# Two graph layers on one core: the diagonal product of the graph numbers starts later, and the last pairs of rows run in another order

## The chip, the cores and the metric

The kernel runs on one core of a Trainium2 chip. The metric is the device time of one execution in microseconds (us), and of several executions the median. TensorE multiplies matrices (a matmul's weights are loaded beside the matmul before it), VectorE and ScalarE do elementwise work, GpSimd does small elementwise work here, and SyncE (SP) issues the DMAs. Each engine works through its own queue in order, and the engines wait for each other's semaphores.

## The reference

x is 2048 x 256, adj is a 2048 x 2048 matrix of zeros and ones. The first layer is graph attention with a gated second branch; the second is attention inside each of 32 graphs, whose bounds stand in ptr. Cut to what matters:

```
h   = relu(layernorm(x))
hs  = h @ W_sa;  s = hs @ a_left [:, None] + hs @ a_right [None, :]
e   = where(adj != 0, exp(-leaky_relu(s, 0.01)), 0)
x_a = e / (sum(e) + 1e-5) @ hs
x_b = adj @ (h @ W_gcnb) + b_gcnb
ga, gb = sigmoid([adj @ h, h] @ Wa.T + ba), sigmoid([adj @ h, h] @ Wb.T + bb)
x1  = x + sigmoid(ga * x_a + gb * x_b)

h1   = relu(layernorm(x1))
q, k, v = h1 @ Wq.T + bq, h1 @ Wk.T + bk, h1 @ Wv.T + bv
mask = graph_id[:, None] == graph_id[None, :]
sc   = (where(mask, q @ k.T / 16, 0) + 2 * adj) * where(mask, 1, -1e6)
out  = x1 + (softmax(sc) * mask) @ v
```

## The kernel before

The 2048 nodes are 16 tiles of 128, or 8 pairs of tiles. Every product of 32-bit numbers is made from 16-bit halves: a high half (made on ScalarE), a low half (the rest, made on VectorE or GpSimd), and three matmuls (high x high, high x low, low x high).

**Start.** `h` is made and turned, then multiplied with the weights (`times_weights`, `times_w_sa`), and `sums` adds up the second branch of the first block of 512 columns (`pair_sums` in the first tiles). Meanwhile VectorE makes `gid`, each node's graph number, and GpSimd's `gid_diag` is the product of the identity with it (L584, 2048 columns); TensorE's `spread_gid` (L1173) uses it much later, in sweep 0, and waits there for `norm_1_made` 3 and `graphs_made` 6. Around 32 us VectorE reduces the first layer's scores to a minimum (L1665), copies the s columns for a transpose (L1667, L1668), reduces the turned minimum (L1670), and makes the low half of `wsa` (L1672). TensorE turns the minimum (L1341), broadcasts it (L1344), turns the s columns (L1076), and goes on with `times_w_sa(0)` (L1053, `three_products`). Then `hd_low` (L1706) and `keep_b` (L1713 copies `tails`, L1714 makes `xb`) empty the banks of PSUM. `hd_low` of all pairs, `keep_b`, and L1761 have their places in VectorE's queue by hand.

**Sweeps 0 to 3.** In sweep k the engines build the attention weights of 512 rows pair by pair (`raw`, `high` on ScalarE, `mask`, `low` on VectorE) and TensorE's `attend` multiplies them with `hd`; `sums` of the next sweep lie between. At the head of sweep k + 1 the rows are finished: `denominators` (with `ga`, L1874), `keep_a`, `mix`, `tanh_mix`, `add_mix` (`add_only`, then `new_moments` for the layer norm), `inv_new_deviation` on GpSimd, `shifts`, and `normalize` on ScalarE with `h1_low` on GpSimd. DMA transposes on SP's queue (`turn_h1`) turn each pair's h1; each waits for `h1_low` of its pair.

**The last pairs.** After pair 5 of sweep 3 every engine follows a list written out by hand. It holds the last 4 tiles of `attend`, the finish of the last 4 tiles of rows (12 to 15), and the second layer's attention, pair by pair: `keys` and `values` (TensorE) wait for the transposes of the pair; `keys_high`, `keys_low`, `values_high`, `keep_values` (which makes `lift`) and `values_low` (GpSimd) keep them; `scores` multiplies; `maxima` (L1958, L1964) gives the row's shift; `exponents` and `turn_p`, `pT_high`, `pT_low` give the weights, `gather` (L1259) multiplies with the values, `outer_part` and `row_sums` (GpSimd) sum up the rest, and `results` (for the last pair `results_last`, L1987) write `o_sb`, which SP stores. These lists are what the change rewrites. A step waits for the numbers of its semaphores: `keys(p)` for the low half of the keys of pair p - 1, `values(p)` for `lift` of pair p - 1, `scores(p)` for the low half of its own pair and, below pair 3, for `keep_a` of row p, since it takes over that bank.

Of the kernel before, what the change touches and what calls it, by code (L numbers as in the profile page):

```python
# [10 lines left out]
ALU = mybir.AluOpType  # L11
# [19 lines left out]
def two_graph_layers(nc, x, adj, adj_t, W_sa, W_saT, a_col, W_gcnb, b_gcnb, gate_w, gate_b, ptr,  # L31
# [4 lines left out]
    NT = N // P  # L36
    KT = D // P
    CT = 4
# [14 lines left out]
    with ExitStack() as ctx:  # L53
# [3 lines left out]
        def sem(name):  # L57
            return ctx.enter_context(nc.semaphore(name))
# [211 lines left out]
        norm_1_summed = sem("norm_1_summed")  # L270
        norm_1_made = sem("norm_1_made")
        inv_1_made = sem("inv_1_made")
# [256 lines left out]
        def _(eng):  # L529
# [53 lines left out]
            eng.wait_ge(graphs_made, 5)  # L583
            eng.tensor_tensor(gid_diag, ident_b[:, :].rearrange("p (a n) -> p a n", a=1).broadcast_to([P, NT, P]),  # L584
# [3 lines left out]
            eng.tensor_tensor(ninv_1[:, :], nsq_1[:, :], half_neg[:, 0:4], ALU.pow).then_inc(inv_1_made, 1)  # L588
# [62 lines left out]
            eng.wait_ge(scale_1_made, SCALES)  # L651
            h1_low(4)
            outside(LAST)
            values_low(0)
            h1_low(5)
            values_low(1)
            inv_new_deviation(CT * LAST, CT * LAST + 2)
            outer_part(0)
            values_low(2)
            outer_part(1)  # L660
            outer_part(2)
            row_sums(0)
            inv_new_deviation(CT * LAST + 2, NT)
            h1_low(6)
            row_sums(1)
# [3 lines left out]
            outer_part(4)  # L669
            h1_low(7)  # L670
            row_sums(3)
            values_low(4)
            values_low(5)
            row_sums(4)
            outer_part(5)
            outer_part(6)
            row_sums(5)
            row_sums(6)
            outer_part(7)
            values_low(6)  # L680
            values_low(7)
            row_sums(NQ - 1)

        @block.scalar
        def _(eng):
# [265 lines left out]
            values_high(1)  # L951
            keep_a(LAST, 0, 2)
            tanh_mix(LAST, 0, 2)
            keys_high(1)
            exponents(0, 0)
            values_high(2)
            exponents(0, 1)
            keep_a(LAST, 2, CT)
            keys_high(2)
            normalize(6)  # L960
            pT_high(0)
            tanh_mix(LAST, 2, CT)
            values_high(3)
            exponents(1, 0)
            exponents(1, 1)
            keys_high(3)
            keys_high(4)
            pT_high(1)
            exponents(2, 0)
            normalize_tile(7, 0)  # L970
            exponents(2, 1)
            keys_high(5)
            pT_high(2)
            exponents(3, 0)
            normalize_tile(7, 1)
            values_high(4)
            exponents(3, 1)
            exponents(4, 0)
            exponents(4, 1)
            values_high(5)  # L980
            pT_high(3)
            pT_high(4)
            keys_high(6)
            exponents(5, 0)
            exponents(5, 1)
            keys_high(7)
            pT_high(5)
            exponents(6, 0)
            exponents(6, 1)
            values_high(6)  # L990
# [42 lines left out]
        def _(eng):  # L1033
# [142 lines left out]
            def norm_1():  # L1176
                eng.wait_ge(sq_1_made, 4)
                eng.matmul(L[:, 0, 0:4], ones[:, :], sq_1[:, :], start=True, stop=True).then_inc(norm_1_summed, 1)
# [211 lines left out]

            values(0, 0)
            values(0, 1)
            attend(LAST, NT - 4, (0, 1))
            attend(LAST, NT - 3, (0, 1))
            values(1, 0)
            values(1, 1)
            attend(LAST, NT - 2, (0, 1))
            attend(LAST, NT - 1, (0, 1))
            attend(LAST, NT - 4, (2, 3))
            values(2, 0)  # L1400
            values(2, 1)
            scores(0)
            keys(1)
            attend(LAST, NT - 3, (2, 3))
            attend(LAST, NT - 2, (2, 3))
            attend(LAST, NT - 1, (2, 3))
            keys(2)
            scores(1)
            values(3, 0)
            values(3, 1)  # L1410
            turn_p(0)
            scores(2)
            keys(3)
            values(4, 0)
            keys(4)
            gather(0)
            turn_p(1)
            values(4, 1)
            scores(3)
            keys(5)  # L1420
            turn_p(2)
            gather(1)
            scores(4)
            values(5, 0)
            values(5, 1)
            keys(6)
            gather(2)
            turn_p(3)
            turn_p(4)
            scores(5)  # L1430
            values(6, 0)
            values(6, 1)
            gather(3)
            keys(7)
            scores(6)
# [67 lines left out]
        def _(eng):  # L1503
# [278 lines left out]
            def norms_1():  # L1782

                eng.wait_ge(norm_1_summed, 1)
# [5 lines left out]
            def scales_1():  # L1790
                eng.wait_ge(inv_1_made, 1)
# [266 lines left out]
            keep_values(1)  # L2058
# [3 lines left out]
            keep_values(2)  # L2062
            maxima(0)
            add_mix(LAST, 0, 2)
            keys_low(1)
            denominators(LAST, 2, CT)
            shifts(NT - 4, NT - 2)
            mix(LAST, 2)
            mix(LAST, 3)
            keys_low(2)  # L2070
            maxima(1)
            keep_values(3)
            maxima(2)
            add_only(LAST, 2, CT)
            pT_low(0)
            new_moments(LAST, 2, CT)
            keys_low(3)
            shifts(NT - 2, NT)
            results(0)
            keys_low(4)  # L2080
            pT_low(1)
            maxima(3)
            keep_values(4)
            keys_low(5)
            maxima(4)
            results(1)
            pT_low(2)
            keep_values(5)
            results(2)
            pT_low(3)  # L2090
            pT_low(4)
            maxima(5)
            keys_low(6)
            results(3)
            keep_values(6)
            maxima(6)
            keys_low(7)
            pT_low(5)
            keep_values(7)
            maxima(7)  # L2100
            results(4)
            pT_low(6)
            results(5)
# [90 lines left out]
```

## Time and profile before

| | us |
|---|---|
| median of 3 executions | 231.44 (230.99 to 233.67) |
| profiled execution, its own time | 232.15 |
| profiled execution, span of the instructions | 230.2 |
| TensorE busy / VectorE / ScalarE / GpSimd | 217.0 / 190.2 / 161.5 / 68.3 |
| mean granted clock of TensorE | 0.992 of full speed |

The span runs from the first to the last instruction; the execution's own time is 1.95 us longer. Busy times are sums over the span and can overlap between the engines. An idle time in brackets behind a row is that of the engine just before it, with the instruction that released it.

### The profile page before, as it was taken

To read this page: it belongs to the slowest core of one execution; us is meant where nothing else is said; L and a number is where in the kernel's file an instruction comes from. 1 tells how busy PE (TensorE), PEld (TensorE's weight loads), DVE (VectorE), ACT (ScalarE), POOL (GpSimd) and SP (SyncE) were. 2 spreads that over 40 slices of the span, in tenths; PEclk is the share of its full clock that TensorE was granted. 3 is DMA by queue.
4 is the path that set the end of the run, shared out by engine and by line. 5 is a ranking of instruction groups with operands and counts; after the bars stand their busy time and mean duration, and the time that the engine had idled before them with its cause. 6 is when DMAs were issued, how large, how long until landed. Compare 5 with 4: busy or idle time off the path is not lost.

```text
span 230.2 us, 5297 instructions
## 1 busy us (share of the span) xinstructions
PE 217.0 (94%) x1974; PEld 187.9 (82%) x1976; DVE 190.2 (83%) x481; ACT 161.5 (70%) x310; POOL 68.3 (30%) x114
## 2 busy tenths in 40 slices
PE   7999989999999999999999999999999989899980
PEld 7878878888888888888888888888788769788850
DVE  2889898989996975699999499987599949899891
ACT  3779735799967434975782795669999845999660
POOL 4643860000026000001800001732124472267470
PEclk9999999999999999999999999999999999999996
DMA  6999499006989300824410000001203131012733
GB/s 194 353 373 382 127 358 362 7 0 211 291 272 391 118 3 0 299 93 157 129 56 3 1 1 3 1 3 39 52 3 68 26 63 30 4 24 42 191 109 99
DMA packets 28796, 28.43 MB, mean 124 GB/s; under 512 B 10593, under 2 KB 20577, under 8 KB 28769
## 3 DMA queue, kind: packets, MB, share of 16 engines
q1 hardware_dynamic: 28080, 27.81, 37.2%
q8 instruction: 16, 0.26, 0.5%
q10 hardware_dynamic: 688, 0.27, 0.5%
q14 instruction: 12, 0.09, 0.1%
HBM read 23.88 MB, written 2.10 MB: 113 GB/s over the span
## 4 chain that ended last, share of the span: by engine, by line
PE 62%; DVE 20%; issue 6%; ACT 5%; DMA 3%; POOL 1%; SPq 1%; DVEq 0%; ACTq 0%; POOLq 0%
PE bank_b L1105 21%; PE bank_a L1053 9%; PE bank_a L1129 9%; PE bank_a L1131 9%; PE bank_a L1133 9%; DVE e_lo L1728 2%; DVE adjt L1919 2%; DVE e_slot L1722 2%; DMA adjt<-in_x 2%; ACT adjt L844 2%; PE bank_l L1045 1%; DVE st6b L1897 1%; DMA adjt<-adjt 1%; DVE x_all L1889 1%; DVE adjt L1999 1%
## 5 line engine op out<-in xcount | busy, mean ns | idle before, releaser
L1131 PE MATMUL bank_a<-hd,e_hi 128*128 128x257 f16 x256 | 70.2, 274 | 0.0
L1129 PE MATMUL bank_a<-hd,e_hi 128*128 128x257 f16 x256 | 69.6, 272 | 0.1
L1133 PE MATMUL bank_a<-hd,e_lo 128*128 128x257 f16 x256 | 69.5, 271 | 0.0
L1105 PE MATMUL bank_b<-hb,adjt 128*128 128x259 f16 (+1 forms) x512 | 66.5, 273 | 0.5 <-DVE hb L1539 0.3
L1105 PEld LDWEIGHTS bank_b<-hb,adjt 128*128 128x128 bf16 x512 | 49.3, 97 | 7.9 <-DVE xb L1714 0.5
L735 ACT ACTIVATE e_hi<-e_slot 128x1024 f16<-128x1024 f32 x32 | 33.6, 1050 | 26.6 <-PE bank_a L1133 15.4
L1722 DVE SCALAR_TENSOR_TENSOR e_slot<-e_slot,adjt 128x1024 f32<-128x1024 f32 x32 | 39.0, 1218 | 8.6 <-ACT e_slot L728 8.6
L1728 DVE SCALAR_TENSOR_TENSOR e_lo<-e_slot,e_hi 128x1024 f16<-128x1024 f32 x32 | 39.0, 1218 | 4.9 <-ACT e_hi L735 4.9
L728 ACT ACTIVATE e_slot<-s_row,nbias 128x512 f32<-128x512 f32 x64 | 42.3, 709 | 0.2
L593 POOL TENSOR_TENSOR rs_all<-veb,half_neg 128x2 f32<-128x2 f32 x8 | 7.4, 930 | 72.8 <-DVE veb L1902 72.8
L1129 PEld LDWEIGHTS bank_a<-hd,e_hi 128*128 128x128 f16 x256 | 24.7, 96 | 4.1 <-issue 0.3
L1133 PEld LDWEIGHTS bank_a<-hd,e_lo 128*128 128x128 f16 x256 | 25.2, 98 | 3.3
L1131 PEld LDWEIGHTS bank_a<-hd,e_hi 128*128 128x128 f16 x256 | 24.6, 96 | 3.7
L844 ACT ACTIVATE adjt<-x_all,nb_all,rs_all 128x256 f32<-128x256 f32 (+1 forms) x32 | 16.6, 591 | 0.4 <-DVE nb_all L1912 0.4
L616 POOL TENSOR_TENSOR adjt<-adjt 128x512 f16<-128x512 f32 x8 | 9.3, 1164 | 20.7 <-ACT adjt L844 20.7
L1053 PE MATMUL bank_b<-w_v,adjt 128*128 128x257 f16 x96 | 12.1, 273 | 1.5 <-DVE lift L1933 1.5
L817 ACT ACTIVATE xa<-bank_a,ga 128x256 f32<-128x256 f32 x16 | 6.4, 475 | 9.6 <-DVE ga L1874 9.6
L1053 PE MATMUL bank_l<-adjt,w_qk 128*128 128x256 f16 x96 | 11.8, 273 | 0.2 <-DMA adjt<-adjt 0.2
L588 POOL TENSOR_TENSOR ninv<-nsq,half_neg 128x4 f32<-128x4 f32 x1 | 1.9, 1930 | 33.6 <-DVE nsq L1788 33.6
L1053 PE MATMUL bank_a<-wb,x_all 128*128 128x262 f16 x96 | 11.8, 274 | 0.0
L1053 PE MATMUL bank_a<-wsa,x_all 128*128 128x256 f16 x96 | 11.6, 272 | 0.0
L1053 PEld LDWEIGHTS bank_b<-w_v,adjt 128*128 128x128 f16 x96 | 9.1, 97 | 3.0 <-issue 1.7
(232 smaller groups left out, 363.4 us busy)
## 6 DMA issues: line engine op xcount, KB each, us to landing
adjt<-in_adj_t SPq DMA_DIRECT2D x16, 1024.0 KB, 9.0
x_all<-in_x SPq DMA_DIRECT2D x4, 512.0 KB, 5.4
out<-adjt SPq DMA_DIRECT2D x16, 128.0 KB, 1.8
adjt<-in_x SPq DMA_DIRECT2D x3, 512.0 KB, 7.3
diag<-in_adj SPq DMA_DIRECT2D x16, 64.0 KB, 3.8
adjt<-in_x SPq DMA_DIRECT2D x2, 256.0 KB, 3.7
e_slot<-in_L_gnn_W_gcnb ACTq DMA_DIRECT2D x1, 256.0 KB, 3.9
e_slot<-in_W_saT SPq DMA_DIRECT2D x1, 256.0 KB, 4.1
```

Of the source, the lines that this page charges most:

```text
L593: eng.tensor_tensor(rs_all[:, first:last], veb[:, r0:r1], half_neg[:, 0:r1 - r0], ALU.pow) \
L616: eng.tensor_tensor(h1n16[:, p % ROWS, :, 1, :], h1[:, p % 2, :, :], h1n16[:, p % ROWS, :, 0, :], ALU.subtract).then_inc(h1_lo_made, 1)
L728: ins = eng.activation(slot_words(g)[:, n * CW:(n + 1) * CW], s_row[:, k * CW:(k + 1) * CW], ACT.Exp, scale=SLOPE - 1.0, bias=nbias[:, j:j ...
L735: eng.activation(high_words(g), slot_words(g), ACT.Copy, scale=E_SCALE).then_inc(hi_ready, 1)
L844: eng.activation(into, x1_all[:, i * D:(i + 1) * D], ACT.Relu, scale=rs_all[:, i:i + 1], bias=nb_all[:, i:i + 1]).then_inc(h1_ready, 1)
L1053: mm = eng.matmul(bank, left(kk, a), right(kk, b), start=(kk == 0 and a + b == 0), stop=(kk == KT - 1 and a == 1))
L1105: eng.matmul(B[:, r % 2, 0:cols], adjt_block(k, j, r), hb16[:, j, part, 0:cols], start=(j == 0 and part == 0), stop=(j == NT - 1 and part ...
L1129: eng.matmul(A[:, r, 0:D + 1], high, hd16[:, j, 0, 0:D + 1], start=(j == 0), stop=False, skip_group_check=True)
L1131: eng.matmul(A[:, r, 0:D + 1], high, hd16[:, j, 1, 0:D + 1], start=False, stop=False, skip_group_check=True)
L1133: mm = eng.matmul(A[:, r, 0:D + 1], low, hd16[:, j, 0, 0:D + 1], start=False, stop=(j == NT - 1), skip_group_check=True)
L1722: eng.scalar_tensor_tensor(out=slot_words(g), in0=slot_words(g), scalar=1.0, in1=adjt_words(k, 2 * q, 0, PW), op0=ALU.min, op1=ALU.mult) \
L1728: eng.scalar_tensor_tensor(out=low_words(g), in0=slot_words(g), scalar=E_SCALE, in1=high_words(g), op0=ALU.mult, op1=ALU.subtract) \
```

## The change

GpSimd waits for `norm_made` 6, which VectorE signals with L1697, before it makes `gid_diag`. Two semaphores are merged into others that count the same instructions. The order of the last pairs is another one on TensorE, ScalarE, VectorE and GpSimd; `normalize`, `keep_a` and `add_mix` are split into their parts at some places, and the steps stay the same. SP's queue is unchanged.

```
@@ gpsimd @@
             eng.wait_ge(graphs_made, 5)
+            eng.wait_ge(norm_made, 6)
             eng.tensor_tensor(gid_diag, ident_b..., gid..., ALU.mult).then_inc(graphs_made, 1)
             eng.wait_ge(norm_1_made, 3)
-            eng.tensor_tensor(ninv_1[:, :], nsq_1[:, :], half_neg[:, 0:4], ALU.pow).then_inc(inv_1_made, 1)
+            eng.tensor_tensor(ninv_1[:, :], nsq_1[:, :], half_neg[:, 0:4], ALU.pow).then_inc(inv_made, 1)
@@ norm_1 (tensor), norms_1 and scales_1 (vector) @@
-  ... .then_inc(norm_1_summed, 1)          -  eng.wait_ge(norm_1_summed, 1)     -  eng.wait_ge(inv_1_made, 1)
+  ... .then_inc(norm_summed, 1)            +  eng.wait_ge(norm_summed, 5)       +  eng.wait_ge(inv_made, 5)
```

The four lists before stand in the listing above; after the change they read, in order:

```
GpSimd:  outside(LAST) h1_low(4) inv_new_deviation(12, 14) outer_part(0) h1_low(5) values_low(0)
         outer_part(1) row_sums(0) row_sums(1) values_low(1) inv_new_deviation(14, 16) h1_low(6)
         outer_part(2) values_low(2) h1_low(7) row_sums(2) outer_part(3) values_low(3) values_low(4)
         values_low(5) outer_part(4) outer_part(5) row_sums(3) row_sums(4) outer_part(6) row_sums(5)
         values_low(6) outer_part(7) values_low(7) row_sums(6) row_sums(7)
ScalarE: keep_a(LAST, 0, 1) keep_a(LAST, 1, 2) tanh_mix(LAST, 0, 2) keys_high(1) keep_a(LAST, 2, 3)
         keep_a(LAST, 3, 4) keys_high(2) normalize_tile(6, 0) exponents(0, 0) exponents(0, 1)
         tanh_mix(LAST, 2, 4) keys_high(3) values_high(1) pT_high(0) exponents(1, 0) exponents(1, 1)
         keys_high(4) values_high(2) pT_high(1) normalize_tile(6, 1) normalize_tile(7, 0)
         exponents(2, 0) exponents(2, 1) normalize_tile(7, 1) keys_high(5) pT_high(2) values_high(3)
         exponents(3, 0) exponents(3, 1) keys_high(6) values_high(4) values_high(5) exponents(4, 0)
         pT_high(3) keys_high(7) exponents(4, 1) exponents(5, 0) pT_high(4) exponents(5, 1)
         pT_high(5) values_high(6) exponents(6, 0) exponents(6, 1) values_high(7) pT_high(6)
         (then as before)
TensorE: attend(tiles 12 to 15, rows 0, 1) values(0) attend(tiles 12 to 15, rows 2, 3) keys(1) keys(2)
         scores(0) values(1) keys(3) turn_p(0) scores(1) values(2) keys(4) gather(0) values(3, 0)
         turn_p(1) scores(2) values(3, 1) keys(5) scores(3) values(4) gather(1) turn_p(2) scores(4)
         keys(6) values(5, 0) turn_p(3) values(5, 1) gather(2) keys(7) scores(5) values(6) turn_p(4)
         scores(6) gather(3) turn_p(5) values(7) (then as before: scores(7) gather(4) turn_p(6) ...)
VectorE: denominators(LAST, 0, 2) mix(0) mix(1) denominators(LAST, 2, 4) add_only(LAST, 0, 2)
         new_moments(LAST, 0, 2) keys_low(1) shifts(12, 14) mix(2) maxima(0) mix(3) keep_values(1)
         keys_low(2) maxima(1) add_only(LAST, 2, 4) pT_low(0) keep_values(2) keys_low(3)
         new_moments(LAST, 2, 4) keys_low(4) shifts(14, 16) keep_values(3) maxima(2) results(0)
         pT_low(1) maxima(3) keep_values(4) results(1) pT_low(2) keys_low(5) maxima(4) keys_low(6)
         keep_values(5) results(2) pT_low(3) maxima(5) keys_low(7) keep_values(6) pT_low(4) maxima(6)
         results(3) pT_low(5) keep_values(7) maxima(7) (then as before: results(4) pT_low(6) ...)
```

## Rows read from the trace of the kernel before

Each row of a timeline has its start, its duration, the engine, the line, the operation, what it writes and reads, and how many instructions.

**Rows 1.** The page: busy time and share of the span of each engine.

```profile
PE 217.0 (94%) x1974; PEld 187.9 (82%) x1976; DVE 190.2 (83%) x481; ACT 161.5 (70%) x310; POOL 68.3 (30%) x114
```

**Rows 2.** TensorE's waits from 44 us on, longest first.

```profile
PE bank_b L1053 <- DVE lift L1933: 1.5, 1, 1.5
```

**Rows 3.** Timelines of GpSimd and VectorE, the product and its neighbours.

```profile
30.56 3.61 POOL L584 TENSOR_TENSOR z_same<-ident_b,gid 128x2048 bf16<-128x2048 bf16 x1 [2.07 <-DVE onehot L1556]
67.75 1.93 POOL L588 TENSOR_TENSOR ninv<-nsq,half_neg 128x4 f32<-128x4 f32 x1 [33.58 <-DVE nsq L1788]
...
31.91 2.29 DVE L1667 COPY s_cols<-hc 128x16 f32<-128x16 f32 x1
34.12 0.18 DVE L1668 COPY s_cols<-hc 128x32 f32<-128x32 f32 x1
34.22 0.27 DVE L1670 TENSOR_REDUCE rm<-bank_l 1x1 f32<-1x128 f32 x1
34.42 0.73 DVE L1672 SCALAR_TENSOR_TENSOR wsa<-e_slot,w_mul,wsa 128x512 f16<-128x512 f32 x1
```

**Rows 4.** Timeline of TensorE from 32 to 36 us.

```profile
32.56 0.27 PE L1341 MATMUL bank_l<-ident,rm 128*1 128x128 f32 x1
...
34.54 0.38 PE L1344 MATMUL bank_l<-rm,ones 1*128 1x1 f32 x2 [0.82 <-DVE rm L1670]
...
35.20 2.79 PE L1053 MATMUL bank_a<-wsa,x_all 128*128 128x256 f16 x24
```

**Rows 5.** Timeline of VectorE from 37 to 42 us.

```profile
37.59 0.15 DVE L1697 TENSOR_TENSOR norm<-norm_sq,norm_inv 128x1 f32<-128x1 f32 x1
...
39.20 0.23 DVE L1713 COPY tails<-bank_b 128x71 f32<-128x71 f32 x1 [0.39 <-PE bank_b L1115]
...
41.05 0.22 DVE L1761 TENSOR_TENSOR hd<-dp_s,hd 128x16 f16<-128x16 f32 x1
```

**Rows 6.** Timelines of GpSimd and VectorE around 213 us.

```profile
212.05 2.28 POOL L621 TENSOR_TENSOR adjt<-adjt 128x512 f16<-128x512 f32 x2
...
212.98 0.74 DVE L1969 SCALAR_TENSOR_TENSOR adjt<-bank_a,adjt 128x256 f16<-128x256 f32 x2
```

**Rows 7.** Timeline of TensorE in the last pairs.

```profile
180.90 0.83 PE L1053 MATMUL bank_b<-w_v,adjt 128*128 128x257 f16 x6
...
198.81 0.84 PE L1217 MATMUL bank_a<-adjt 128*128 128x128 f16 x12 [1.12 <-DVE adjt L1919]
199.49 1.47 PE L1053 MATMUL bank_l<-adjt,w_qk 128*128 128x256 f16 x12
200.80 0.83 PE L1053 MATMUL bank_b<-w_v,adjt 128*128 128x257 f16 x6
201.46 1.47 PE L1053 MATMUL bank_l<-adjt,w_qk 128*128 128x256 f16 x12
...
203.43 0.38 PE L1226 MATMUL bank_a<-ident,adjt 128*128 128x128 f32 x2
203.65 0.72 PE L1053 MATMUL bank_b<-w_v,adjt 128*128 128x257 f16 x5
```

**Rows 8.** Timelines of GpSimd and VectorE: ga beside GpSimd's work and without it.

```profile
195.07 1.16 POOL L621 TENSOR_TENSOR adjt<-adjt 128x512 f16<-128x512 f32 x1
...
160.93 0.22 DVE L1874 SCALAR_TENSOR_TENSOR ga<-rden,norm,gates 128x4 f32<-128x4 f32 x1
...
195.27 0.97 DVE L1874 SCALAR_TENSOR_TENSOR ga<-rden,norm,gates 128x2 f32<-128x2 f32 x1
```

**Rows 9.** The chain that ended last, at the last pair's transposes.

```profile
210.16 1.12 POOL adjt L616
...
212.53 2.81 DMA adjt<-adjt
```

**Rows 10.** Timelines of TensorE and VectorE: the last scores and the last result.

```profile
219.19 0.51 PE L1217 MATMUL bank_a<-adjt 128*128 128x128 f16 x6
...
225.05 0.47 DVE L1987 SCALAR_TENSOR_TENSOR adjt<-bank_a,rz,x_all 128x256 f32<-128x256 f32 x1
```

More of the change, by code:

```diff
@@ L668, in _ @@
             values_low(3)
[L669 to L671 removed]
             values_low(4)
             values_low(5)
+            outer_part(4)
+            outer_part(5)
+            row_sums(3)
             row_sums(4)
[L675 removed]
             outer_part(6)
             row_sums(5)
+            values_low(6)
+            outer_part(7)
+            values_low(7)
             row_sums(6)
[L679 to L682, printed above, removed]
+            row_sums(7)
         @block.scalar
@@ L1177, in norm_1 @@
                 eng.wait_ge(sq_1_made, 4)
-                eng.matmul(L[:, 0, 0:4], ones[:, :], sq_1[:, :], start=True, stop=True).then_inc(norm_1_summed, 1)
+                eng.matmul(L[:, 0, 0:4], ones[:, :], sq_1[:, :], start=True, stop=True).then_inc(norm_summed, 1)
             def keys(p):
@@ L1388, in _ @@
                         attend(k, 1)
+            attend(LAST, NT - 4, (0, 1))
+            attend(LAST, NT - 3, (0, 1))
+            attend(LAST, NT - 2, (0, 1))
+            attend(LAST, NT - 1, (0, 1))
             values(0, 0)
             values(0, 1)
[L1393 to L1398, printed above, removed]
             attend(LAST, NT - 4, (2, 3))
[L1400 to L1403, printed above, removed]
             attend(LAST, NT - 3, (2, 3))
@@ L1406, in _ @@
             attend(LAST, NT - 1, (2, 3))
+            keys(1)
             keys(2)
-            scores(1)
[L1409 to L1414, printed above, removed]
+            scores(0)
+            values(1, 0)
+            values(1, 1)
+            keys(3)
+            turn_p(0)
+            scores(1)
+            values(2, 0)
+            values(2, 1)
             keys(4)
             gather(0)
+            values(3, 0)
             turn_p(1)
+            scores(2)
+            values(3, 1)
+            keys(5)
+            scores(3)
+            values(4, 0)
             values(4, 1)
-            scores(3)
-            keys(5)
+            gather(1)
             turn_p(2)
-            gather(1)
             scores(4)
+            keys(6)
             values(5, 0)
+            turn_p(3)
             values(5, 1)
-            keys(6)
             gather(2)
-            turn_p(3)
-            turn_p(4)
+            keys(7)
             scores(5)
@@ L1432, in _ @@
             values(6, 1)
+            turn_p(4)
+            scores(6)
             gather(3)
-            keys(7)
-            scores(6)
             turn_p(5)
@@ L2061, in _ @@
             mix(LAST, 1)
-            keep_values(2)
-            maxima(0)
-            add_mix(LAST, 0, 2)
+            denominators(LAST, 2, CT)
+            add_only(LAST, 0, 2)
+            new_moments(LAST, 0, 2)
             keys_low(1)
-            denominators(LAST, 2, CT)
             shifts(NT - 4, NT - 2)
             mix(LAST, 2)
+            maxima(0)
             mix(LAST, 3)
+            keep_values(1)
             keys_low(2)
             maxima(1)
+            add_only(LAST, 2, CT)
+            pT_low(0)
+            keep_values(2)
+            keys_low(3)
+            new_moments(LAST, 2, CT)
+            keys_low(4)
+            shifts(NT - 2, NT)
             keep_values(3)
             maxima(2)
[L2074 to L2078, printed above, removed]
             results(0)
-            keys_low(4)
             pT_low(1)
```

75 lines of the change are left out of this document (38 added, 37 removed).

## The prediction

> **What bounds the kernel now.** I first read the busy shares on the page, to see that TensorE works 94% of the span [rows 1]. So only idle time on TensorE, the start and the end can be saved. Next come TensorE's waits from 44 us on, to see how few they are: the largest are 1.5 us, for `lift` of VectorE, and 1.1 us, for the low half of the keys [rows 2, 7]. Both lie in the last pairs. The third view is the timeline of GpSimd and VectorE around 30 us. The diagonal product runs 3.61 us from 30.56, and a copy of 16 columns that starts at 31.91 takes 2.29 us and ends at 34.20, just when the product ends [rows 3]. TensorE's timeline shows who pays: the broadcast of the minimum starts at 34.54 after 0.82 us idle, released by the reduction that stands behind the copy [rows 4]. From 44 us to about 180 us TensorE has no wait that the view lists, so what it wins at 34 us should reach the end.
>
> **Part 1, the product held back.** `gid_diag` now waits for `norm_made` 6, which L1697 signals. The copy then costs what its neighbour of 32 columns does, 0.18 us [rows 3]. The reduction L1670 is limited instead by TensorE's transpose L1341, 32.56 + 0.27 = 32.83 [rows 3, 4]. Reduction (0.27) and wsa's low half (0.73) then end at about 33.85, where they ended at 35.15 before. TensorE reaches the broadcast at 34.54 - 0.82 = 33.72, when its minimum is ready (33.1), and `times_w_sa(0)` (35.20 before, behind 0.66 us of broadcast and transpose) comes at 34.38, later than 33.85 [rows 4]. The whole 0.82 us goes, and nothing takes its place: gain 0.82 us.
>
> Where does the product land? L1697 stood at 37.59 [rows 5]. VectorE's chain in front of it gains the 0.82 us of TensorE's transpose of the s columns and somewhat more, so I put it at 36.3 and the product at 36.4 to 40.0. Bounds: free if nothing on VectorE wants the port then; at worst the product's own 3.61 us, less the time nothing waits. What stands there on VectorE is `hd_low` and `keep_b`, which read PSUM and one SBUF tensor. Steps of that form are not slowed: two `pT_low` take 0.74 us inside 2.28 us of GpSimd work [rows 6]. The next step with two SBUF tensors is L1761, at 41.05 - 0.82 = 40.23, 0.2 us after the product [rows 5]. I take zero. Behind the new wait GpSimd has nothing until `ninv_1` at 67.75, after 33.58 us of idleness, and TensorE's `spread_gid`, which uses the product, also waits for `norm_1_made` 3, the very thing that released `ninv_1` [rows 3]. SP's queue is not touched. The merged semaphores (`norm_summed` 5, `inv_made` 5) count the same instructions: zero.
>
> One step under the product has no twin in the trace: the copy of `tails` from PSUM (L1713, 39.20) [rows 5]. If it took the port, it would wait from 38.38 to 40.04, and TensorE's later wait for `xb` with it: 1.66 us. I take zero, for the other PSUM readers of rows 6. The Trainium skill ("VectorE: DVE Perf Modes", Mode 2×_2P) says that a copy with a PSUM source can't use both ports, since PSUM has one VectorE read port; by that rule this risk is nil; no row here shows it for a copy.
>
> **Part 2, the last pairs.** The set of steps is the same on every engine (`add_mix`, `normalize`, `keep_a` are only split), so TensorE's work between its first changed step at 180.90 and `scores(7)` at 219.19 is fixed. From start to start [rows 7]: scores 0.68, keys 1.31, half of values 0.66 (0.11 a matmul of 257 columns), gather 203.43 - 201.46 - 1.31 = 0.66, turn 0.22. There are 48 matmuls of `attend` (5.3), 16 halves of values (10.6), 7 keys (9.2), 7 scores (4.7), 6 turns (1.3), 4 gathers (2.6): 33.7 us. 38.29 us pass, so TensorE stands idle 4.55 us there. That is the ceiling of part 2.
>
> What makes the idleness? GpSimd's long steps read SBUF, and VectorE's steps with two SBUF tensors stand still beside them: `ga` took 0.22 us alone and 0.97 us when it met `values_low` [rows 8]. That `ga` holds up `keep_a`, `mix` and the keys of pair 2, for which `scores(2)` waited 1.12 us [rows 7]. The 1.5 us wait is that of `values(1)`, which stands so early that `keep_values(0)` isn't done [rows 2].
>
> For the rest I laid the four queues side by side: each step starts when its engine is free and its semaphores are there 0.04 us after the signal, durations as in the timelines of this profile, and a step with two SBUF tensors on VectorE and a reader on GpSimd exclude each other. Laid out so, the old order ends at 225.99, where the trace has its last result at 225.05 + 0.47 = 225.52 [rows 10], and `scores(7)` at 219.66, where it was 219.19. Without the exclusion it would end at 222.9, 2.6 us too early: the port is a real part of the loss.
>
> The new order gives TensorE: `attend` of rows 0, 1 to 183.56 (the low half that its third step needs is there at 181.8, the step comes at 182.2), `values(0)` to 184.89, rows 2, 3 to 187.55, keys 1 and 2 to 190.17, `scores(0)`, `values(1)`, keys 3, then 0.23 us of waiting for pair 0's exponents. VectorE has `ga` at 186.2 and 188.2 with GpSimd idle from 185.7 to 190.6; its steps are no longer blocked until 195.4, and then by 0.1 us. `lift` of pair 0 comes at 185.9, `values(1)` only at 190.84. TensorE reaches keys 6 at 204.96. Their transposes depend on `h1_low(6)`, at 200.39 in the new order. A pair of transposes lands 4.05 us after `h1_low` ends (210.16 + 1.12, then 212.53 + 2.81 = 215.34) [rows 9]: at 205.63, a wait of 0.68 us. Keys 7 wait 0.13 us in the same way. All in all 1.04 us idle, `scores(7)` at 180.90 + 33.74 + 1.04 = 215.68. That is 3.51 us earlier. From there to the last result it was 6.33 us [rows 10]; laid out it is 6.39, since GpSimd's order of the last sums differs. Gain 3.45 us.
>
> Bounds of part 2: all idleness gone, 4.5 us; or the 4.05 us of a transpose grow, each of them one for one (at 4.9 instead of 4.05 the end is 0.85 later).
>
> By the Trainium skill ("SBUF — State Buffer", Who interferes with whom) a `tensor_scalar` from SBUF to SBUF can hold both ports too. In the new order this meets the small step `veb` of tiles 14, 15 at 199.05, beside `values_low(1)`: 0.25 us later there, 0.06 us at the end, so the gain would be 4.21 instead of 4.27. No row here shows it for a `tensor_scalar`; for the copy of rows 3 the trace agrees.
>
> **The sum.** 0.82 + 3.45 = 4.27 us. The profiled execution took 232.15 us (span 230.2), so 227.9; it was 0.71 us above the median, 231.44, so for the median 227.2.
>
> **Rivals.**
> - All waits go. The layout made the old order 0.47 us too long, so it may overstate the new one too. With no idleness at all: 0.82 + 4.49 = 5.31, 226.1. Against it: the transposes' latency is a measured floor.
> - Held back in vain. The copy's 2.29 us ends with the product, which speaks for the port; if it stood still for another reason, 0.82 stays: 228.0. If the `tails` copy takes the port at the new place: 227.2 + 1.66 = 228.9.
> - The new order makes waits of its own. ScalarE has two runs without a break (197.4 to 201.3 and 201.9 to 206.6), and each wait of one pair holds the next pair's behind it. If this gives back 2 of the 3.45 us: 229.2.
> - Slower. One mechanism: the layer norm of tiles 13 to 15 now stands on ScalarE behind the exponents and the turn of pair 1, and `new_moments` of tiles 14, 15 on VectorE behind the turn of pair 0. Is that chain late, `h1_low(6)` and (7) are late, the transposes land late, and keys 6 and 7 stop TensorE one for one. Against it: the layout has them late by only 0.68 and 0.13 us. It decides from 4.3 us of further lateness on; at 5.3 us the time is 232.5.
>
> **How the numbers follow.** A difference under 2% (4.6 us) is about what a measurement of this kernel can't tell from none; 226.8 is the bound. Chances: forecast 227.2 (226.4 to 228.2) 0.56; all waits go 0.12; in vain or the copy blocked 0.13; new waits 0.15; slower 0.04. The range 226.0 to 229.8 leaves out the slow case and the edges of the two neighbours. Faster by over 2%: the 0.12 and nearly half of the forecast's own range, 0.35. Slower by over 2% (236.1) needs 9 us of stalls: 0.02. The rest, 0.63.
>
> **What the changed profile would show.** Right: the copy L1667 near 0.2 us; no idle time before the broadcast L1344; the product at about 36.4, 3.6 us long, `tails` copies beside it at 0.23 us; both `ga` of the last pairs at 0.2 us; about 1 us of TensorE waits from 180 us to `scores(7)`, most before keys 6 and 7 and released by DMA; `scores(7)` 4.3 us earlier. Wrong: a long L1713 or L1706 under the product, a wait of TensorE for `xb` above 0.2 us; waits for ScalarE's exponents or keys' high halves; `h1_low(6)` more than 1 us behind the end of pair 1's exponents; or a lower granted clock after a stall.

## The result and the profile after

The changed kernel takes 228.28 us (median of 4 runs, 227.96 to 228.85), the kernel before 231.57 us (median of 4 runs beside it). The ratio is 0.985, interval 0.980 to 0.989: 3.3 us faster, inside the range, 1.1 us more than the 227.2 us forecast. The profiled execution took 228.31 us, span 226.5.

The page of the changed kernel, busy time by engine. TensorE's work is the same (216.7 us against 217.0), VectorE's is 4.3 us less [rows 1]. It has as many instructions as before (481), so its steps only stand still less.

```profile
PE 216.7 (96%) x1974; PEld 189.0 (83%) x1976; DVE 185.9 (82%) x481; ACT 161.4 (71%) x310; POOL 68.5 (30%) x114
```

VectorE and GpSimd of the changed kernel around the place the product left, and around its new one (timelines; the code stands two lines further down than before for VectorE and TensorE, so L1667 is now L1669):

```profile
32.15 0.16 DVE L1669 COPY s_cols<-hc 128x16 f32<-128x16 f32 x1
32.23 0.18 DVE L1670 COPY s_cols<-hc 128x32 f32<-128x32 f32 x1
33.11 0.28 DVE L1672 TENSOR_REDUCE rm<-bank_l 1x1 f32<-1x128 f32 x1 [0.70 <-PE bank_l L1343]
33.32 0.73 DVE L1674 SCALAR_TENSOR_TENSOR wsa<-e_slot,w_mul,wsa 128x512 f16<-128x512 f32 x1
...
38.35 0.23 DVE L1715 COPY tails<-bank_b 128x71 f32<-128x71 f32 x1 [0.63 <-PE bank_b L1117]
...
40.20 0.29 DVE L1763 TENSOR_TENSOR hd<-dp_s,hd 128x16 f16<-128x16 f32 x1
```
```profile
36.79 3.61 POOL L583 TENSOR_TENSOR z_same<-ident_b,gid 128x2048 bf16<-128x2048 bf16 x1 [8.05 <-DVE norm L1699]
```

The copy fell from 2.29 to 0.16 us [rows 3], and the reduction behind it is ended by TensorE's transpose, as forecast. The product stands at 36.79 to 40.40. Both things that lie under it are to be read here: the copy of `tails`, which reads PSUM, takes 0.23 us as before [rows 5], and the step with two SBUF tensors that just touches its end takes 0.29 instead of 0.22 us.

TensorE of the changed kernel at the same place (timeline). No idle time stands before the broadcast, and `times_w_sa` comes 0.83 us earlier [rows 4], though the transpose in front (32.80) was 0.24 us later than in the run of before:

```profile
32.80 0.27 PE L1343 MATMUL bank_l<-ident,rm 128*1 128x128 f32 x1
...
33.89 0.38 PE L1346 MATMUL bank_l<-rm,ones 1*128 1x1 f32 x2
...
34.37 2.78 PE L1055 MATMUL bank_a<-wsa,x_all 128*128 128x256 f16 x24
```

TensorE's waits from 44 us on (in total, how many, the longest), and its timeline in the last pairs:

```profile
PE bank_l L1055 <- DMA adjt<-adjt: 2.1, 2, 1.4
PE bank_a L1228 <- ACT adjt L867: 0.5, 1, 0.5
PE bank_l L1237 <- ACT adjt L867: 0.3, 1, 0.3
PE bank_b L1246 <- DVE adjt L1978: 0.2, 1, 0.2
```
```profile
193.27 0.44 PE L1228 MATMUL bank_a<-ident,adjt 128*128 128x128 f32 x2 [0.49 <-ACT adjt L867]
...
205.46 0.72 PE L1055 MATMUL bank_l<-adjt,w_qk 128*128 128x256 f16 x5 [0.72 <-DMA adjt<-adjt]
...
210.56 1.48 PE L1055 MATMUL bank_l<-adjt,w_qk 128*128 128x256 f16 x12 [1.41 <-DMA adjt<-adjt]
...
216.97 0.83 PE L1219 MATMUL bank_a<-adjt 128*128 128x128 f16 x12
```

The waits for `lift` and for the low half of the keys [rows 2, 7] are gone. Three are left before `scores(7)` (216.97): `turn_p(0)` for the exponents, keys 6 and keys 7 for their transposes. The chain that ended last shows keys 7's (start, duration):

```profile
203.67 1.17 POOL adjt L615
204.85 1.19 SPq L510
206.09 4.42 DMA adjt<-adjt
210.56 1.48 PE bank_l L1055 x12
```

Before, the first and the last of these took 1.12 and 2.81 us [rows 9], and the link on SP 1.19 us as now. It is the DMA that is 1.61 us longer.

The last result (VectorE's timeline) comes at 222.93 + 0.48 = 223.41, where it was 225.52 [rows 10]: 2.11 us earlier. The span is 3.7 us shorter. The difference lies behind the last result, in SP's stores; two timelines, before and after:

```profile
214.14 12.69 SPq L464 DMA_DIRECT2D out<-adjt  x16
```
```profile
207.40 16.47 SPq L462 DMA_DIRECT2D out<-adjt  x16
```

Before, the last issue ends at 226.83, 1.31 us behind the last result; after, at 223.87, 0.46 us behind. From the last result to the end of the span it is 4.68 us before and 3.09 after. This isn't the change's doing: three of the experiments below keep the old order of the last pairs and have 3.1 us there (the first: span 228.7, last result 225.65). The profiled execution of before was 1.6 us longer behind its last result than theirs; why isn't shown.

### The profile page after: what moved, and what is told of

It is laid out like the page before. It is cut to its first block, busy times and chain, and to the rows that moved or that the text cites. A ratio compares the mean times of both kernels' runs of the same rounds, so it can differ in the third digit from the quotient of the medians.

```text
span 226.5 us, 5300 instructions
## 1 busy us (share of the span) xinstructions
PE 216.7 (96%) x1974; PEld 189.0 (83%) x1976; DVE 185.9 (82%) x481; ACT 161.4 (71%) x310; POOL 68.5 (30%) x114
## 4 chain that ended last, share of the span: by engine, by line
PE 82%; DVE 7%; issue 3%; POOL 2%; ACT 2%; DMA 2%; SPq 1%; DVEq 0%; POOLq 0%; ACTq 0%
PE bank_b L1107 25%; PE bank_a L1131 12%; PE bank_a L1133 12%; PE bank_a L1135 12%; PE bank_a L1055 9%; PE bank_a L1281 2%; DMA adjt<-adjt 2%; PE bank_l L1055 2%; PE bank_b L1055 2%; PE bank_l L1047 1%; DVE adjt L2001 1%; PE bank_a L1219 1%; PE bank_b L1149 1%; DVE adjt L1960 1%; DVE adjt L1933 1%
## 5 line engine op out<-in xcount | busy, mean ns | idle before, releaser
L1055 PEld LDWEIGHTS bank_l<-adjt,w_qk 128*128 128x128 f16 x96 | 9.2, 97 | 3.7 <-DMA adjt<-adjt 2.6
L1055 PEld LDWEIGHTS bank_a<-wb,x_all 128*128 128x128 f16 x96 | 9.2, 98 | 1.5 <-DVE norm_sq L1651 0.2
```

What stands on the lines that cost most here:

```text
L1055: mm = eng.matmul(bank, left(kk, a), right(kk, b), start=(kk == 0 and a + b == 0), stop=(kk == KT - 1 and a == 1))
```

## The experiments

Each time is the median, beside runs of the kernel before in the same job (231.22 us for the first four, 231.11 for the next four, 231.32 for the last three); ratios are to those, with the 95% interval in brackets. Each trace is of one execution, so a time in it can differ from the median.

**1 and 2. The two parts alone.** Part 1 alone is one line in the kernel before; part 2 alone is the changed kernel without it.

```diff
+            eng.wait_ge(norm_made, 6)
             eng.tensor_tensor(gid_diag, ident_b[:, :].rearrange("p (a n) -> p a n", a=1).broadcast_to([P, NT, P]),
```

> The kernel before with the held-back product alone. Theory of the port: the copy of 16 columns falls from 2.29 us to under 0.2, the idle 0.82 us in front of the broadcast is gone, and TensorE's first step of the last pairs comes 0.8 to 0.9 us earlier (180.90 before): time 0.8 us lower, 0.3%. The rest of the saving belongs to the new order. Rival, that the head start is given back later: the same head start at 44 us, but the last result not earlier than 225.3 us. Rival, that the product does harm at its new place: a tails copy or an xb step over 1 us long.

> The changed kernel without the wait that holds the product back. If the parts add up: about 2.5 us faster than before (3.3 less 0.8), the copy long again (about 2.3 us), 0.8 us idle before the broadcast, and in the last pairs the same waits as in the changed kernel (0.5, 0.7 and 1.4 us). Rival, that the parts need each other: no faster than 1.5 us.

Measured: part 1 alone 230.12 us, ratio 0.995 (0.992 to 0.999), so 1.1 us faster. Part 2 alone 228.50 us, 0.989 (0.985 to 0.993), 2.7 us faster. Both together were 3.3 us faster, less than the sum, 3.8; each interval is wider than that difference, so it isn't shown that the parts fail to add up. The traces say where something may go. Part 1 alone, VectorE's copy and TensorE's keys 7:

```profile
32.27 0.16 DVE L1668 COPY s_cols<-hc 128x16 f32<-128x16 f32 x1
```
```profile
215.50 1.49 PE L1054 MATMUL bank_l<-adjt,w_qk 128*128 128x256 f16 x12 [1.05 <-DMA adjt<-adjt]
```

Part 2 alone, the same two:

```profile
32.17 2.30 DVE L1668 COPY s_cols<-hc 128x16 f32<-128x16 f32 x1
```
```profile
210.50 1.49 PE L1054 MATMUL bank_l<-adjt,w_qk 128*128 128x256 f16 x12 [0.36 <-DMA adjt<-adjt]
```

The copy is short with the hold and long without it, in any order of the pairs. But keys 7 start at 210.50 without the hold and at 210.56 with it: in the changed kernel the wait there is 1.05 us longer. Part 2 alone, the chain at the last transpose:

```profile
205.96 1.19 SPq L510
207.20 3.25 DMA adjt<-adjt
```

With the hold this transpose is issued at 206.09, 1.11 us earlier, so GpSimd and SP had kept the head start. The transfer lost it: 4.42 us against 3.25. Experiments 6 and 7 show why. In part 1 alone the profiled execution gives the whole head start back at keys 7: its last result is at 225.65, against 225.52 before, which is the sign named for the first rival. The median is 1.1 us lower all the same, as the theory had it, so on where the head start of part 1 alone ends up trace and median disagree.

**3. The stores held back.** In the changed kernel SP issues the first stores at 207.40, before keys 7's transposes land. If the stores hold those up, then it helps to wait.

```diff
+            eng.wait_ge(h1_turned[1], turned(NQ - 1))
```

(on SP, between the last transposes and the first store)

> The changed kernel, and SP's queue waits for the last pair's transposes before the first store of a result. In the changed kernel the second transpose of the last pair landed 4.42 us after its issue, where 2.4 to 3.4 us was seen before, and the first stores were issued 1.3 us behind it. Theory of the collision: the stores' packets hold it up; now it lands within 2.9 us, keys(7) waits 0 to 0.2 us instead of 1.41, scores(7) comes 1.2 to 1.4 us earlier, and the time is 1.0 to 1.4 us below the changed kernel's. Rival, the DMA queue is slow by itself there (a fetch of instructions, or two transposes behind one another): still 3.5 us or more to landing, and the time unchanged. Rival, the stores come too late: transposes on time, but the span's end 1 us or more further behind the last result.

Measured: 227.92 us, ratio 0.985 (0.981 to 0.988), as the changed kernel. The stores' row on SP and TensorE's keys 7:

```profile
210.35 13.34 SPq L462 DMA_DIRECT2D out<-adjt  x16
```
```profile
210.38 1.48 PE L1056 MATMUL bank_l<-adjt,w_qk 128*128 128x256 f16 x12 [1.21 <-DMA adjt<-adjt]
```

No store is under way any more and the second transpose still lands 4.1 us after its issue. That the stores delay it is refuted.

**4. The copy as a reduction.** In the kernel before, the two copies are written as sums over an axis of one element; the product stays where it was.

```diff
-            eng.tensor_copy(s_cols[:, 0, 0:NT], hc[:, :, 2]).then_inc(s_parts_made, 1)
-            eng.tensor_copy(s_cols[:, 2:4, 0:NT], across(hc[:, :, 2], [P, 2, NT])).then_inc(s_parts_made, 1)
+            eng.tensor_reduce(s_cols[:, 0, 0:NT], hc[:, :, 2:3], AX, ALU.add).then_inc(s_parts_made, 1)
+            for n in (2, 3):
+                ins = eng.tensor_reduce(s_cols[:, n, 0:NT], hc[:, :, 2:3], AX, ALU.add)
+            ins.then_inc(s_parts_made, 1)
```

> The kernel before with the product where it was, and the two copies of the s columns made by additions over an axis of one element, which read one tensor and give the same numbers (three instructions instead of two). Theory of the port: a reduction needs no second port; each takes under 0.25 us beside the product, the 0.82 us wait before the broadcast is gone, time 0.7 to 0.8 us lower than before, just as in the run with the product held back. Rival, any read of SBUF on VectorE is held up by the product, or the columns' stride is what is slow: the first reduction takes over 1 us, and the time doesn't change.

Measured: 230.51 us, 0.998 (0.994 to 1.001). GpSimd's product and VectorE beside it:

```profile
31.20 3.61 POOL L584 TENSOR_TENSOR z_same<-ident_b,gid 128x2048 bf16<-128x2048 bf16 x1 [2.09 <-DVE onehot L1556]
```
```profile
32.53 0.17 DVE L1667 TENSOR_REDUCE s_cols<-hc 128x16 f32<-128x16 f32 x1
32.62 0.26 DVE L1669 TENSOR_REDUCE s_cols<-hc 128x16 f32<-128x16 f32 x2
...
33.71 1.65 DVE L1674 SCALAR_TENSOR_TENSOR wsa<-e_slot,w_mul,wsa 128x512 f16<-128x512 f32 x1
```

The same 16 columns move in 0.17 us in the middle of the product: it is the kind of instruction that stood still, not the data or the place. But the next step, with two SBUF tensors, now meets the product and takes 1.65 instead of 0.73 us; it ends at 35.36, and TensorE waits 0.50 us for it. Of the 0.82 us saved, the trace gives 0.50 back, so on TensorE a cheaper copy alone wins about 0.3 us: the product has to go from there. The median is 0.7 us lower, as the theory forecast, but the interval reaches no change at all and doesn't tell 0.3 from 0.8. The Trainium skill ("SBUF — State Buffer", Who interferes with whom) says just this of the two: a reduction can't enter a mode with two ports and never contends, a step with two inputs in SBUF contends with GpSimd's reads. The trace agrees with both, 0.17 and 1.65 us.

**5. One swap on GpSimd.** In the kernel before, `values_low(2)` goes behind `outer_part(1)`, so that no long GpSimd step meets the second `ga`.

```diff
             outer_part(0)
-            values_low(2)
             outer_part(1)
+            values_low(2)
```

> The kernel before with one step moved on GpSimd: values_low(2) behind outer_part(1), so that it no longer runs beside the second ga of the last pairs. Theory of the port: that ga takes 0.22 us instead of 0.97, keep_a, the keys' halves of pair 2 and scores(2) come 0.7 us earlier, so TensorE's 1.12 us wait there falls to about 0.4; the other waits stay, and the last result is up to 0.7 us earlier if the last transposes don't take it back. Rival, ga is long for another reason (two tiny operands on partitions that ScalarE reads): it stays near 0.9 us and so does the 1.12 us wait.

Measured: 230.77 us, 1.000 (0.996 to 1.004). VectorE's two `ga` and TensorE's `scores(2)`:

```profile
188.78 0.74 DVE L1874 SCALAR_TENSOR_TENSOR ga<-rden,norm,gates 128x2 f32<-128x2 f32 x1
195.42 0.22 DVE L1874 SCALAR_TENSOR_TENSOR ga<-rden,norm,gates 128x2 f32<-128x2 f32 x1
```
```profile
198.21 0.84 PE L1217 MATMUL bank_a<-adjt 128*128 128x128 f16 x12 [0.38 <-DVE adjt L1919]
```

The second `ga` fell from 0.97 to 0.22 us and `scores(2)`'s wait from 1.12 to 0.38 us [rows 7, 8], so the cause of that wait is shown. In the profiled execution the last result comes 0.94 us earlier (224.58). But that execution (229.46 us) is the fastest of the twelve; the median is 0.3 us below the kernel before, and the ratio shows no gain. So what the wait's end is worth at the end of the kernel stays open.

**6 and 7. The instructions' fetch.** What is beside keys 7's transposes? In the views of the DMA queues there is one packet of instructions (queue 8) every 11 to 18 us from 180 us on. They are TensorE's: the waits put on its queue below move them against the work. The changed kernel from 207.6 to 208.2 us:

```profile
DMA packets 347, 0.10 MB, mean 163 GB/s; under 512 B 346, under 2 KB 346, under 8 KB 346
...
q1 hardware_dynamic: 346, 0.08, 67.6%
q8 instruction: 1, 0.02, 14.2%
```

Of 347 packets all but one are the transposes' small ones, and the one takes 14.2% of 16 x 0.6 us, 1.4 us of a DMA engine's time. To move it against the work I put waits that are always satisfied at TensorE's start: 24 in one kernel, 66 in the other.

```diff
+            for _ in range(24):
+                eng.wait_ge(consts_made, 1)
```

> The changed kernel with 24 waits more at TensorE's start, on a semaphore that is already there. They compute nothing; they move the places at which TensorE's instructions are fetched by 24 instructions, so each fetch comes about 1.3 us earlier. In the changed kernel one fetch (one packet on one DMA engine, near 208.2 us) falls together with the last pair's second transpose (its packets at 207.3 to 208.1), which then trickles on until 210.5. Theory of the fetch: here the packet comes near 206.9 us, still within the transposes, and the landing stays late (3.5 us or more after its issue) and the time within 0.5 us of the changed kernel. Rival, the transposes are slow there by themselves: the landing stays late in this and in the run with 66 waits.

> The same with 66 waits: the fetch comes about 3.6 us earlier, near 204.6 us, in the gap between the transposes of pairs 6 and 7. Theory of the fetch: the last transpose lands 2.4 to 2.9 us after its issue, keys(7) waits under 0.2 us instead of 1.41, and the time is 1.0 to 1.4 us below the changed kernel's. Rival, slow by themselves: landing 3.5 us or more, time unchanged. Rival, the fetch only moves onto pair 6's transposes: keys(6) waits over 1.5 us instead of 0.72, and the time doesn't change.

Measured: with 24 waits 228.9 us, 0.990 (0.987 to 0.993); with 66 waits 233.56 us, 1.009 (1.006 to 1.0125). So the second is 5.3 us slower than the changed kernel, where its expectation said 1.0 to 1.4 us faster. The waits weren't free. The broadcast before `times_w_sa` (33.89 in the changed kernel) stands at 34.53 and at 36.94, that is 0.64 and 3.05 us later (in the profiles with the hold and without these waits it stands anywhere from 33.60 to 34.11), so the packet (at 207.8 both times, where 206.9 and 204.6 were expected) is 0.8 and 3.2 us earlier against the work, not in the time of the trace. With 66 it hits another pair: keys 6's transposes land late and keys 7's in time. The chain of the kernel with 66 waits, and its DMA issues from 210 to 212 us, the last transpose among them (2.5 us to landing):

```profile
204.26 1.19 SPq L510
205.88 4.05 DMA adjt<-adjt
209.97 2.09 PE bank_l L1055 x12
```
```profile
adjt<-adjt SPq DMA_TRANSPOSE x1, 2.5
```

So the late landing went with the packet from one pair to the other: of the expectation for 66 waits, keys 7's part came true, and so did the last rival (keys 6 wait 2.19 us). Over the profiles of before, of the changed kernel and of experiments 1 to 7 (packet's start in windows of 0.2 us; issue of the transposes from SP's rows or in windows of 0.3 us; both in us), for the transposes of pairs 6 and 7:

| kernel | packet | late transposes: issue, landing after | the others of these pairs |
|---|---|---|---|
| before | 212.0 | 211.3: 3.4; 212.5: 2.8 | 2.4 to 2.5 |
| part 1 alone | 211.2 | 210.6: 3.5 | 2.4 to 2.5 |
| changed | 208.0 | 206.1: 4.4 | 2.4 to 2.6 |
| part 2 alone | 207.8 | 205.7: 4.0; 207.2: 3.3 | 2.4 to 2.5 |
| stores held back | 207.8 | 206.3: 4.1 | 2.4 |
| 24 waits | 207.8 | 206.7: 3.9 | 2.4 to 2.5 |
| 66 waits | 207.8 | 205.9: 4.0 | 2.4 to 2.5 |
| reduction | 210.0 | none under way | 2.4 to 2.5 |
| GpSimd swap | 209.4 | none under way | 2.4 to 2.5 |

In the two kernels where the packet falls between the pairs no transpose is late. The earlier pairs show the same. In the changed kernel the second transpose of pair 5 (issued at 194.94) meets the packet before; nothing waits for it yet, and keys 5 start at 199.73 without a wait. The row of its issue and the row of the packet (window 196.6 to 196.8 us):

```profile
adjt<-adjt SPq DMA_TRANSPOSE x1, 4.2
```
```profile
q8 instruction: 1, 0.02, 27.4%
```

The traces of all thirteen profiles hold 208 transposes. 30 of them landed 2.8 to 4.4 us after their issue, and with each of these a packet of queue 8 was under way between issue and landing. The other 178 took 2.4 to 2.6 us; only two of them meet such a packet, one in its own last 0.07 us, and for the other the packet is over (208.8) before SP is done issuing it (209.2). With the 66 waits that moved packet and lateness together, this shows the packet as the cause. It also shows what the landing follows. 26 of the 30 were issued before the packet began, from 0.6 to 2.4 us before, and all of these landed 2.0 to 3.1 us after the packet's start. So an earlier issue gains little there: without the hold the last transpose had 0.7 us from issue to packet, with it 2.0, and it landed at 210.5 in both. Why the landing takes 2.0 us or more from the packet's start isn't explained; the packet's own time is 0.9 to 1.4 us. The Trainium skill ("Runtime: NRT & Kernel Launch", Instruction fetch mechanics) says that each engine's sequencer fetches its instructions by DMA in blocks of 16 KiB, 256 instructions, and calls the cost mostly hidden; the row's 0.02 MB fits the block, the table doesn't fit "hidden": none of TensorE's listed waits is for instructions, but a transfer that it waits for is late.

The 66 waits cost more than their 3.05 us. TensorE stood still for 2.35 us before 209.97, and 0.7 us later its granted clock fell (windows of 1 us; behind the stretch PE, PEld, DVE, ACT and POOL busy, then the granted clock):

```profile
209.00:210.00 1.00, 0.03 (x1) 0.03 (x2) 0.95 (x6) 0.19 (x3) 0.97 (x1) 1.00 0.65 131
210.00:211.00 1.00, 1.00 (x8) 0.82 (x9) 0.00 (x0) 0.00 (x0) 0.00 (x0) 0.84 0.49 100
211.00:212.00 1.00, 1.00 (x6) 0.72 (x5) 0.00 (x0) 0.00 (x0) 0.00 (x0) 0.50 0.49 145
...
213.00:214.00 1.00, 1.00 (x6) 0.82 (x5) 0.85 (x2) 0.46 (x1) 0.46 (x1) 0.50 0.43 143
214.00:215.00 1.00, 1.00 (x10) 0.89 (x9) 0.30 (x1) 0.00 (x0) 0.69 (x1) 0.95 0.00 0
```

From about 210.7 to 214.1 it is 0.5, the 1.2 GHz level. Keys there take 2.09 instead of 1.48 us, half of values 1.50 instead of 0.83, the turn 0.63 instead of 0.38, the next half 1.08 instead of 0.83: 1.8 us together. With 3.05 at the start, 2.35 - 0.88 at keys 6 and -1.57 at keys 7 this makes 4.7 us; the last result is 4.6 us later (227.98).

**8 to 11. A third order with slack before the transposes.** If the transposes' landing is what is left, TensorE should have other work while it waits. The steps of the last pairs in a third order, the hold kept (TensorE's list, cut to the parts that matter; the other three lists are rearranged to suit):

```diff
+            turn_p(2)
             values(4, 0)
             values(4, 1)
             gather(1)
-            turn_p(2)
             scores(4)
-            keys(6)
             values(5, 0)
-            turn_p(3)
             values(5, 1)
+            keys(6)
+            turn_p(3)
             gather(2)
-            keys(7)
             scores(5)
             values(6, 0)
             values(6, 1)
             turn_p(4)
+            keys(7)
             scores(6)
```

> The changed kernel with the four lists of the last pairs in a third order, the same steps: laid out as in the prediction, but with the transposes taken once at 4.05 us and once at 5.2 us, and an order looked for that ends early with either. The normalized tiles of pairs 6 and 7 and their low halves stand further in front, keys(6) and keys(7) further behind. If late transposes are what the changed kernel still pays (0.72 + 1.41 us), TensorE waits under 0.5 us in all between 180 us and scores(7), the last result comes 1.3 to 2 us earlier than the changed kernel's 223.4, and the time is 1.2 to 2 us lower, about 226.5. Rival, the layout is wrong in what it doesn't know (ScalarE without a gap): new waits for exponents or halves of over 1 us, and no gain.

Measured: 226.17 us (225.78 to 226.32), 0.977 (0.973 to 0.982). That is the best of all kernels here. The list has no wait of TensorE between 44 us and `scores(7)` (214.03, where the changed kernel has 216.97). Behind it two waits are longer, 1.01 us for ScalarE's exponents (0.29 in the changed kernel) and 0.49 us for VectorE (0.23), so the last result, at 221.29, is 2.1 us earlier and not 2.9. To see it beside the changed kernel, and to see what the hold is worth where TensorE doesn't wait for transposes, three more: the third order without the hold, the third order again, the changed kernel again.

```diff
-            eng.wait_ge(norm_made, 6)
```

> The third order of the last pairs (e8_dma_slack) with the product not held back. Theory: in the changed kernel the 0.83 us won at the front is swallowed by the wait of keys 7 for its transposes, whose landing is fixed by GpSimd, SP and the DMA and not by TensorE; where that wait is gone, as in the third order, the front's 0.83 us reaches the end. So without the hold the copy takes 2.3 us again, TensorE waits 0.83 us at the minimum's broadcast, every step of the last pairs stands 0.8 us later than in e8_dma_slack and the last result comes at 221.29 + 0.8 = 222.1; median about 0.8 us (0.35%) above the third order with the hold. Rival: the front's gain is swallowed at any rate (something before the last pairs absorbs it): last result within 0.2 us of 221.3 and the same median.

> The third order with the hold once more, beside the changed kernel on the same chip. Theory: 226.2 us again, 2.1 us (0.9%) below the changed kernel, since TensorE waits 0.2 us before scores(7)'s predecessors instead of 3.1 us, most of the difference at keys 6 and 7. Rival: the 2.1 us between two jobs were the chips' difference; then the two kernels lie within 0.3%.

> The changed kernel itself once more: 228.3 us, 1.5% below the kernel before. Theory of the instruction fetch: a 16 KB packet of TensorE's instructions falls at about 208.0 us, beside the transposes for keys 7, and they land more than 4 us after their issue instead of 2.4 to 2.5; keys 7 waits 1.2 to 1.5 us. Rival: the late landing is chance and differs from run to run; then it is 2.5 us here and the wait is below 0.3 us.

Measured, in one job: third order 226.23 us, 0.976 (0.972 to 0.981); without the hold 227.13 us, 0.980 (0.976 to 0.985); the changed kernel 228.22 us, 0.984 (0.979 to 0.989). The third order's slowest of 6 runs (226.59) is faster than the changed kernel's fastest (226.66) and than the fastest without the hold (226.90). Keys 7 in the third order, in the changed kernel again, and the broadcast without the hold:

```profile
209.83 1.48 PE L1055 MATMUL bank_l<-adjt,w_qk 128*128 128x256 f16 x12
```
```profile
210.08 1.48 PE L1055 MATMUL bank_l<-adjt,w_qk 128*128 128x256 f16 x12 [1.21 <-DMA adjt<-adjt]
```
```profile
34.82 0.38 PE L1345 MATMUL bank_l<-rm,ones 1*128 1x1 f32 x2 [0.83 <-DVE rm L1671]
```

In both a transpose lands 4.2 us after its issue beside the packet (207.4, 207.6); the third order has work for TensorE until 0.2 us before that, and the list shows no wait. The late landing repeats in the changed kernel (4.4 and 4.2 us). And here the hold is worth 0.9 us, the 0.83 us of the broadcast: with the wait at keys 7 gone, what is won at 34 us reaches the end.

## Why the prediction was right, and where it wasn't

**Part 1** was right in each step on VectorE and TensorE: copy 0.16 us (0.18 forecast), no idle time before the broadcast, 0.83 us won (0.82), the product at 36.79 (36.4) and nothing harmed by it: `tails` 0.23 us, TensorE's wait for `xb` 0.22 us, the same as before. Experiment 2 shows that the hold does it, experiment 4 that the copy waits for something that a reduction doesn't. Both forms of the rival "held back in vain" are refuted. The first step changed on TensorE came 0.85 us earlier (180.05).

**Part 2** was right in its cause: both `ga` take 0.22 us, the waits for `lift` and for the keys' low half are gone, and the two waits for transposes come where they were put. It failed in the term "lands 4.05 us after `h1_low` ends". For keys 6 the wait was 0.72 us (0.68 forecast), but in part by luck: `h1_low(6)` started at 200.03, where the forecast with the head start taken off is 199.57, the landing came 0.6 us late by the same reckoning, and TensorE was itself 0.4 us late there. For keys 7 it took 5.67 us from the end of `h1_low(7)` (204.84) to 210.51, and the wait was 1.41 instead of 0.13 us. I had taken the 2.81 us of one row as the DMA's own time; the runs show 2.4 to 2.6 us without the instruction packet and 2.8 to 4.4 beside it, so even the row was a disturbed one. `turn_p(0)` waited 0.49 instead of 0.23 us. The three waits make 2.62 us, 1.58 more than forecast. From start to start TensorE loses another 0.16 us at each listed wait, 0.48 together. So `scores(7)` should stand 2.06 us behind its forecast place, which with the head start is 214.86, and it is 2.11 behind.

**The sum.** 4.27 us were forecast for the last result, 2.11 came: 0.85 of head start, 1.37 between the first changed step and `scores(7)` (38.29 us before, 36.92 after), less 0.11 behind `scores(7)`. The median still moved by 3.3 us. The profiled execution of before isn't its median one (0.71 us above it, and with 1.6 us more behind the last result than the other kernels with its order), so the two traces don't place the remaining 1.2 us. What the runs add: those of before spread over 3.4 us (229.99 to 233.35 in 29 runs), those of the third order over 0.8. Which waits of the kernel before vary isn't shown. So the closeness of 228.28 to 227.2 is partly luck, two misses of opposite sign: the last result gained 2.2 us less than forecast, and the median gained 1.2 us more than the last result.

**The sum's form** was wrong too. The parts were added in full. The front's gain only reaches the end if nothing later is set by something that didn't gain. The transposes for keys 7, whose landing follows the instruction packet, stand between. In the third order the hold is worth 0.9 us, measured side by side. In the old order it is 1.1 (the interval allows 0.3 to 1.9). In the changed order the medians of different jobs give 0.2 to 0.3 us (228.50 to 228.28 and 228.22), too little to be told from none: that the hold's gain is swallowed there rests on the traces (1.41 us of waiting at keys 7 with the hold, 0.36 without).

**Rivals.** Waits of the new order's own came, but mostly for the DMA; of the 2.1 us that they gave back only 0.26 are ScalarE's (`turn_p(0)`). So the rival "new waits" was right in its size, with the wrong place. The slow rival's place, keys 6 and 7 stopped by late transposes, was the right one, with another cause: by the prediction's figures `h1_low(7)` ends at 205.22 - 0.82 = 204.40, so it was 0.44 us later than forecast, and the DMA behind it 1.6. The number of the rival "all waits go", 226.1, is about what the third order comes to (226.2), which has none before `scores(7)` but longer ones behind it.

## What to carry to other kernels

Where GpSimd has a long elementwise step from SBUF, look under it for VectorE's copies and two-tensor steps in SBUF: here moving the GpSimd step was better than rewriting the victim, since the next one was caught instead. Before parts of a gain are added, ask what lies between them and the end that is fed by a DMA: a stretch that a transfer sets swallows whatever was won ahead of it, and the cure is to put other work in front of the consumer. A transfer's latency is not one number; take it from all its rows, and plan with the longest.

## What the hardware showed

- Under a 3.61 us GpSimd product a copy of 128x16 fp32 from SBUF to SBUF took 2.29 us (0.16 alone) and a step with two SBUF tensors 1.65 us (0.73 alone). A reduction from SBUF (0.17 us) and a copy from PSUM (0.23 us) were not slowed.
- A DMA transpose of this kernel landed 2.4 to 2.6 us after its issue, but 2.8 to 4.4 us where one packet of TensorE's instructions fell beside it (30 of 208). Issued before such a packet began, it landed 2.0 to 3.1 us after the packet's start.
- Satisfied waits at TensorE's start were not free: with 66 of them the work stood 3.05 us later (46 ns each), with 24 of them 0.64 us, where profiles without them differ by up to 0.5 us at that place.
- 0.7 us after the end of a stall of 2.35 us TensorE's granted clock fell to 0.5, for 3.4 us. In the changed kernel, with stalls of 1.57 us and less in the last pairs, it stayed at 1.0 there.
